# The last block of an attention and experts kernel: an early half projection, zero products, rounded products first, one add on GpSimd

## What is computed

```python
h = layernorm(x) * (1 + ca) + sa
q, k, v = split(h @ W_attn + b_attn)                 # 16 heads of 16
phi = exp(x_head @ omega - |x_head|^2 / 2)           # 128 features
y = (phi_q . cumsum(phi_k v)) / (phi_q . cumsum(phi_k) + eps)
x = x + ga * (y @ W_proj + b_proj)
h = layernorm(x) * (1 + cb) + sb
w = the two largest of softmax(h @ Wg.T + bg), else 0
out = sum over experts e: w[e] * (relu(h @ Wi.T + (h @ A[e].T) @ B[e].T) @ Wo.T)
x = x + gb * out
```

## Time and profile before

| what | value |
| --- | --- |
| median of 3 runs | 759.66 us (759.54 to 762.26) |
| the profiled execution | 758.48 us, its span 756.4 us |
| TensorE matmul busy | 736.2 us, 97% of the span |
| DVE busy | 517.0 us, 68% |
| ScalarE busy | 428.4 us, 57% |
| GpSimd busy | 72.2 us, 10% |

### The profile page before, as it was taken

The page is one execution under the profiler, slowest core; times in us unless marked ns, Lnnn a source line. Parts: engine busy times, 40 slices in busy tenths (PEclk is TensorE's granted clock), DMA queues, the critical chain, the costliest instruction groups (busy, mean ns, idle before and its releaser), DMA issues.

```text
span 756.4 us, 16898 instructions
## 1 busy us (share of the span) xinstructions
PE 736.2 (97%) x6074; PEld 594.8 (79%) x6074; DVE 517.0 (68%) x1255; ACT 428.4 (57%) x775; POOL 72.2 (10%) x81
## 2 busy tenths in 40 slices
PE   8999999999999999999999999999999999999697
PEld 5778779887788868887698877987788876988466
DVE  5647777577667777677766776667766777666566
ACT  4767455765566646665547655666366645565232
POOL 0560200002000110002000020000200010000200
PEclk9999999999999999999999999999999999999899
DMA  9750660107410272104701064101731038000000
GB/s 308 230 116 2 167 155 21 35 28 199 92 55 0 83 184 52 55 0 141 178 0 55 28 194 97 55 0 58 185 75 55 0 118 190 11 30 27 3 1 29
DMA packets 33929, 62.66 MB, mean 83 GB/s; under 512 B 3694, under 2 KB 17874, under 8 KB 33842
## 3 DMA queue, kind: packets, MB, share of 16 engines
q1 hardware_dynamic: 33334, 61.09, 30.7%
q10 hardware_dynamic: 576, 1.31, 0.5%
HBM read 40.37 MB, written 22.02 MB: 82 GB/s over the span
## 4 chain that ended last, share of the span: by engine, by line
PE 87%; DVE 5%; DMA 3%; SPq 2%; ACT 1%; issue 1%; POOL 0%; ACTq 0%; DVEq 0%
PE pa L535 13%; PE ring L658 11%; PE prod L548 7%; PE ring L514 6%; PE pa L410 5%; PE pa L411 5%; PE pa L412 5%; PE ring L568 4%; PE pa L646 4%; PE ring L519 3%; DMA xq<-norm_parts 3%; PE ring L732 2%; PE ring L575 2%; PE prod L514 2%; PE ring L724 2%; PE ring L680 2%
## 5 line engine op out<-in xcount | busy, mean ns | idle before, releaser
L1169 DVE TENSOR_TENSOR am_phk<-pa,const 128x512 f32<-128x512 f32 x112 | 77.1, 689 | 44.3 <-PE pa L535 43.5
L535 PE MATMUL pa<-phq,phkT 128*128 128x128 f32 x768 | 101.2, 275 | 0.0
L535 PEld LDWEIGHTS pa<-phq,phkT 128*128 128x128 f32 x768 | 95.4, 191 | 2.1
L1348 DVE SCALAR_TENSOR_TENSOR am_phk<-ring,am_phk 128x512 f32<-128x512 f32 x64 | 44.1, 689 | 48.2 <-PE ring L732 48.2
L514 PE MATMUL ring<-xq,omega_x 100*128 100x512 f32 x198 | 71.1, 439 | 2.6 <-DMA xq<-norm_parts 1.6
L410 PE MATMUL pa<-wo_r,qk_r 128*128 128x256 f32 x256 | 72.1, 282 | 0.6 <-DVE qk_l L1353 0.6
L411 PE MATMUL pa<-wo_r,qk_l 128*128 128x256 f32 x256 | 72.0, 281 | 0.0
L412 PE MATMUL pa<-wo_l,qk_r 128*128 128x256 f32 x256 | 71.9, 281 | 0.0
L897 ACT ACTIVATE phq<-ring 128x512 f32<-128x512 f32 x84 | 50.6, 602 | 37.4 <-PE ring L514 36.3
L975 ACT ACTIVATE qk_r<-phq 128x512 fp32r<-128x512 f32 x64 | 40.5, 633 | 49.9 <-DVE phq L1357 49.9
L897 ACT ACTIVATE phkT<-ring 128x512 f32<-128x512 f32 x98 | 58.3, 595 | 13.3 <-PE ring L514 12.9
(11 more groups left out here) (201 smaller groups left out, 1596.3 us busy)
## 6 DMA issues: line engine op xcount, KB each, us to landing
xq<-qk_parts SPq DMA_DIRECT2D x45, 512.0 KB
qk_parts<-qk_r SPq DMA_DIRECT2D x32, 256.0 KB, 3.6
qk_parts<-qk_l SPq DMA_DIRECT2D x32, 256.0 KB, 3.9
xr<-in_L_attn_x SPq DMA_DIRECT2D x8, 512.0 KB, 3.5
out_x<-tg SPq DMA_DIRECT2D x16, 256.0 KB, 2.2
tok<-in_L_attn_x SPq DMA_DIRECT2D x7, 512.0 KB, 3.5
phq<-in_L_wmod SPq DMA_DIRECT2D x2, 512.0 KB, 7.4
am_phk<-in_wi_columns SPq DMA_DIRECT2D x2, 512.0 KB, 8.9
```

The source lines that it names most:

```text
L535: mm = pe.matmul(score_bank(q, a)[:, tt], phkT[:, q % 2, a, tt], query(q)[:, a, tt], start=True, stop=True)
L1169: dve.tensor_tensor(am[:, 2 * (q % 2) + a, :].rearrange("p (c t) -> p c t", c=NT), score_bank(q, a)[:].rearrange("p (c t) -> p c t", c=NT) ...
L1348: dve.scalar_tensor_tensor(r2[:, f % 2, :], z_bank[f % 4][:], 0.0, rho, ALU.max, ALU.mult).then_inc(r2_done.sem, 1)
```

## The change

All of it concerns the last block.

1. y's first half is transposed ahead of the last `state_transpose` and copied by ScalarE behind its last copy of products. Its share of the projection is formed in two parts: the first pair of tiles ahead of the last `state_reads`, the second pair ahead of the last `out_transpose`. Behind the attention only k = 1 is left.
2. Three calls of the zero product (`warm(3)`) stand behind the projection.
3. In the last two chunks TensorE takes the eight products of the rounded sums first (`late_output`) and then the four of the difference, each set with a wait of its own. DVE forms the last chunk's sum before the difference of the chunk before it.
4. In `finish` GpSimd adds x to the first pair of tiles, and SyncE waits for it by the new signal `last_first`.

The first hunk is on SyncE, then come TensorE, ScalarE (`copy`), DVE (`late`, `continue`) and GpSimd. `last_stores` is called in place of `ffn_stores` for the last block.

```diff
+            def last_stores(n):
+                    if b == 0:
+                        sp.wait_ge(last_first.sem, 1)
+                    else:
+                        wait(sp, fin, n, 1)
...
                     out_transpose(n, gr - 1)
+                    if q >= PAIRS and not front_next:
+                        y_transpose(n, 0)
...
+                if not front_next:
+                    project(n, 0, 0)
                 state_reads(n, GROUPS - 1)
                 if front_next:
                     qk(n + 1, 2, [1])
+                else:
+                    project(n, 1, 0)
                 out_transpose(n, GROUPS - 1)
...
+                for half in range(2):
+                    for k in range(KT) if front_next else (1,):
+                        project(n, half, k)
...
+            def late_output(n, k):
+                out_of = lambda t: pa[t // 2][:, t % 2 * C:(t % 2 + 1) * C]
+                wait(pe, g_high, n, k + 1)
+                for t in range(NT):
+                    for w in (wo_r, wo_l):
+                        pe.matmul(out_of(t), g_r[:, k % 3, t * P:(t + 1) * P], w[:, k, :], start=False, stop=False,
+                                  skip_group_check=True)
+                wait(pe, g_low, n, k + 1)
+                for t in range(NT):
+                    mm = pe.matmul(out_of(t), g_l[:, k % 3, t * P:(t + 1) * P], wo_r[:, k, :], start=False,
+                                   stop=k == FT - 1, skip_group_check=True)
+                    if k == FT - 1 and t == 1:
+                        mm.then_inc(wo_first.sem, 1)
+                mm.then_inc(wo_mm.sem, 1)
...
-                        wait(pe, g_low, n, k + 1)
+                        if front_next or k < FT - 2:
+                            wait(pe, g_low, n, k + 1)
+                        else:
+                            late_output(n, k)
+                            continue
...
                     qk(n + 1, 3, [1])
                     values(n + 1)
+                else:
+                    warm(3)
                 ffn_head(n, front_next)
...
                     copy(gr)
+                    if gr == GROUPS - 1 and not front_next:
+                        y_copy(n, [0])
...
+                late = FT if front_next else FT - 1
...
-                    if f >= 1:
-                        k = f - 1
-                        wait(dve, g_high, n, k + 1)
-                        dve.tensor_tensor(g_l[:, k % 3, :], g[:, k % 4, :], g_r[:, k % 3, :].bitcast(F32),
-                                          ALU.subtract).then_inc(g_low.sem, 1)
+                    if f >= 1 and f != late:
+                        low_gated(n, f - 1)
                     if f < FT:
                         wait(dve, r2_done, n, f + 1)
                         dve.tensor_tensor(g[:, f % 4, :], g[:, f % 4, :], r2[:, f % 2, :],
                                           ALU.add).then_inc(g_sum.sem, 1)
+                    if f == late:
+                        low_gated(n, f - 1)
...
+                    if b == 0 and not front_next:
+                        continue
                     wait(dve, scaled, n + 1, 2 * b + 2)
...
             rstd_by_halves(NB - 1)
+            wait(pool, scaled, NB, 2)
+            pool.tensor_tensor(tg[:, 0, :], tg[:, 0, :], xr[:, 0:2, :].rearrange("p t c -> p (t c)"),
+                               ALU.add).then_inc(last_first.sem, 1)
```

More of the change, by code:

```diff
@@ L257, in build @@
         oT_added, o_ps, y_step = sig("oT_added", GROUPS), sig("o_ps", GROUPS), sig("y_step", 3 * GROUPS)
+        last_first = sig("last_first")
         mod2_set, mod1_set, mod2c_set = sig("mod2_set", 1), sig("mod1_set", 1), sig("mod2c_set", 2)
@@ L388, in ffn_stores @@
                                  tg[:, b, :].rearrange("p (t c) -> p t c", t=2)).then_inc(out_done.sem, 16)
+            def last_stores(n):
+                dst = block_rows(out_rows, n)
+                for b in range(2):
+                    if b == 0:
+                        sp.wait_ge(last_first.sem, 1)
+                    else:
+                        wait(sp, fin, n, 1)
+                    sp.dma_start(dst[:, 2 * b:2 * b + 2, :],
+                                 tg[:, b, :].rearrange("p (t c) -> p t c", t=2)).then_inc(out_done.sem, 16)
             first_front()
@@ L400, in _ @@
             load_xr(NB - 1)
-            ffn_stores(NB - 1)
+            last_stores(NB - 1)
             wait(sp, out_done, NB, out_done.per)
@@ L638, in projection, with project @@
                     wait(pe, qk_split, n + 1, 2)
+                for half in range(2):
+                    for k in range(KT) if front_next else (1,):
+                        project(n, half, k)
+            def project(n, half, k):
                 row = n // BLOCKS_PER_ROW
[L640 to L647, removed]
+                wait(pe, yT_done, n, k + 1)
+                w = wp_ga[:, row, k, :] if isinstance(n, int) else \
+                    wp_ga[:, bass.ds(row, 1), k, :].rearrange("p o c -> p (o c)")
+                for t in (2 * half, 2 * half + 1):
+                    mm = pe.matmul(pa[half][:, t % 2 * C:(t % 2 + 1) * C], yT[:, k, t * P:(t + 1) * P], w,
+                                   start=k == 0 and t % 2 == 0, stop=k == KT - 1, skip_group_check=True)
+                if k == KT - 1:
                     mm.then_inc(prj_ps.sem, 1)
@@ L788, in after_attend @@
             def after_attend(n, front_next):
-                y_transpose(n, 0)
                 if front_next:
+                    y_transpose(n, 0)
                     qk(n + 1, 3, [0])
@@ L924, in attend, with y_copy @@
                                 front_hT(n + 1)
-            def y_copy(n):
-                for k in range(KT):
+            def y_copy(n, ks):
+                for k in ks:
                     wait(act, yT_ps, n, k + 1)
@@ L1002, in after_attend @@
                     front_qk(n + 1, 2)
-                y_copy(n)
+                y_copy(n, range(KT) if front_next else [1])
                 if front_next:
@@ L1341, in mask_low, with experts @@
                 dve.tensor_tensor(low_both, low, pa[1][0:LROWS], ALU.mult).then_inc(low_masked.sem, 1)
-            def experts(n):
+            def experts(n, front_next):
                 wait(dve, rho_done, n, 1)
+                late = FT if front_next else FT - 1
                 for f in range(FT + 1):
@@ L1358, in experts, with low_gated, finish @@
                                           ALU.add).then_inc(g_sum.sem, 1)
-            def finish(n):
+                    if f == late:
+                        low_gated(n, f - 1)
+            def low_gated(n, k):
+                wait(dve, g_high, n, k + 1)
+                dve.tensor_tensor(g_l[:, k % 3, :], g[:, k % 4, :], g_r[:, k % 3, :].bitcast(F32),
+                                  ALU.subtract).then_inc(g_low.sem, 1)
+            def finish(n, front_next):
                 for b in range(2):
@@ L1383, in ffn_rest @@
                 dve.reciprocal(w1[:], wsum[:]).then_inc(rt.sem, 1)
-                experts(n)
-                finish(n)
+                experts(n, front_next)
+                finish(n, front_next)
             setup_constants()
```

## The result

The changed kernel took 754.9 us (median of 4 executions, 754.69 to 757.15) beside 760.5 for the kernel before, timed with it. The ratio is 0.9947, interval 0.993 to 0.9964: 0.53% or, on the 759.66 shown above, 4.0 us faster, which gives 755.6. Its profiled execution was the longest of the four, 757.15 with a span of 754.8; the other three spans are 752.3 to 752.5. That difference of 2.3 to 2.5 us within one kernel is as large as what the change was forecast to bring, and most of the experiments are about it.

A forecast was written before the change was run, and what follows sets the result against it. TensorE holds 87% of the last-ending chain, so the question was how much of the last block's roughly 50 us is waiting. 1.0 + 0.1 + 0.7 + 0.6 = 2.4 us off 759.66 gives 757.3 us; range 755.3 to 760.2.

The forecast's parts named there:

- the two terms that hang on the clock: Last block: gain of 1.0 us at the attention's end and 0.7 us at the logits, from TensorE's clock staying up.
- the first rival: Last block: clock stays up throughout, logits save 1.8 us, gain 3.55, 756.1 us; chance 0.2.
- the forecast's own case: Ahead of or in the logits: a clock fall costs part of their 1.80 us saving, 0.7 taken; chance 0.35.
- The attention's end: Last block: early half projection fills idle TensorE, last transposes take 0.66 us each, residual starts about 708.7; gain 1.0 us.
- bounds of 0.2 and 1.0: Attention's end: gain 0.2 us from fewer instructions behind the copy alone, up to 1.0 if the clock also stays up.
- The 0.2 for less work behind the copy: Attention's end: four instead of eight instructions behind ACT's copy bring DVE's first projected pair at 709.5, not 709.70.
- The zeros: Behind the projection: three zero calls cost nothing at full clock and save 0.7 us of a possible 1.80 at the logits.
- My ground for 0.7: Ahead of the logits: four microseconds nearly empty, only eight transposes, is closer to what made the clock fall before.
- the end of that cover: Layernorm's transposes: zeros are hidden if over by 712.55; at the low clock they take 5.4 us, over 2 us late.
- The tail: Last two chunks to end: new order and GpSimd's add together gain 0.6 us; bounds 0 and 1.1.
- 0.57: Tail: rounded products first give DVE its first half at 750.2, not 750.77; gain stated as 0.6 us, bounds 0 and 0.7.
- the two causes that I gave: Tail: second store's data queues behind the first's; DVE's last add may wait for GpSimd's until 752.5, ending at 753.2.

The follow-up runs named there:

- e4: Kernel before with the tail alone: order of the last two chunks and GpSimd's add with its store; ratio to before 0.9991 (0.9976 to 1.0006).
- e2: Kernel before with the three zero products behind the projection and nothing else; ratio to before 0.9963 (0.9946 to 0.9981).
- e8: Kernel before with the new order of the last two chunks alone, both adds on VectorE; ratio to before 1.0001 (0.9977 to 1.0025).
- e10: Changed kernel with the early half projection replaced by one zero product in each of its two places; ratio to before 0.9955 (0.9938 to 0.9971).
- e3: Kernel before with the early half projection alone; ratio to before 0.9976 (0.9963 to 0.999).
- e11: Changed kernel with six zero products, warm(6), in place of three; ratio to before 0.996 (0.9941 to 0.9979).
- e5: Changed kernel with the first pair's add back on VectorE; ratio to before 0.9926 (0.9897 to 0.9954).
- e6: Changed kernel with 24 transposes of the identity in place of the three zero products; ratio to before 0.9945 (0.9927 to 0.9963).
- e1: Changed kernel without the three zero products; ratio to before 0.998 (0.9963 to 0.9998).
- e9: Changed kernel timed again without any edit, on another chip; ratio to before 0.9949 (0.9929 to 0.997), median span 754.95 us.

## Why the prediction was right in kind and short in size

The forecast was 2.4 us faster with a part of the logits at the low clock; measured are 4.0 by the ratio (2.7 to 5.3 by its interval). The time was in the range when the ratio is put on the 759.66 shown; the changed kernel's own median of 754.9 is 0.4 below it. So it is the width of the range that held, not its middle: the two terms that hang on the clock came out too small against most of the traces. Most traces went by the first rival, the clock up throughout the last block, for which I had 756.1 and a chance of 0.2; the forecast's own case, a fall that costs part of the logits, is in the first trace alone, where the clock fell at 716.1 and 0.2 of the 1.8 were saved.

*The attention's end, 1.0 forecast, 0.9 to 2.5 measured.* The mechanism is right step by step: 0.66 for 1.12 and 1.11, the residual 0.1 behind GpSimd's add. The sum was made against one execution in which the low clock ended as the projection started (12.95 to the residual). Of the four traces with the old attention end three are longer, 13.89, 14.54 and 14.54: there the clock is back only behind most of the projection (at 710.4, 711.5 and 710.6 in e4, e2 and e8), not at 707.8, at its start. The new end takes 12.06 to 12.18 in nine of ten traces (e10's filled one among them), 12.75 in e3. That bounds of 0.2 and 1.0 were taken from one trace of a clock that I myself had called not tied to the program is the step that failed: the upper bound should have been 2.5. The 0.2 for less work behind the copy is nothing (e10).

*The zeros, 0.7 of 1.8 forecast.* The term of the sum that was mis-sized. Of the eight traces with zeros ahead of the layernorm, seven have the logits at 2.02, one (the changed kernel's first) at 3.59; of the five without, none. So it was worth 1.8 in seven traces of eight and 0.2 in one. My ground for 0.7, that the 4 us ahead of the logits are nearly empty, was not borne out: in these seven traces the clock stayed up through them. That the zeros are hidden was right: 2.74 us for six, over before the first transposes in the changed kernel; and so was the end of that cover (e11).

*The tail, 0.6 forecast, 0.5 measured.* 0.57 was worked out for the order, 4.54 to 4.03 came, and all of it reaches the end (e8). For GpSimd's add little was left in my sum; it is 0.02 to 0.14 (e5). Of the two causes that I gave, the queue of the second store's data fits the rows of e5 (2.4 us to landing instead of 2.1). The DVE add that comes second was delayed by 0.38 us; the data of the store in front covers that, by the same rows, but no run takes the delay away alone. The two stores were issued about 0.55 us apart, not within 0.5.

*Two readings of mine.* The clock is back at 721.4, not at 721.2: the last row is low for most of its half microsecond. Nothing hangs on it. And that no row has the DVE add second is wrong. Setup has one, DVE's L1163 with two SBUF operands, begun inside a GpSimd instruction that reads SBUF:

```profile
26.48 1.95 POOL L1448 TENSOR_SCALAR tok<-xr 128x512 f32<-128x512 f32 x1 [15.93 <-ACT xr L837]
27.37 1.23 DVE L1163 TENSOR_TENSOR wo_l<-am_phk,wo_r 128x1024 fp32r<-128x1024 f32 x1 [1.25 <-ACT wo_r L876]
```

It takes 1.23 us, undisturbed 1.22 (the same line at 24.06), so here it did not wait at all.

*The Trainium skill on both points.* "TensorE: Matmul & The Clock Gate", Part 4, has it that transposes don't count for the clock as matmuls do. The runs are against it: in e6 24 transposes stand where the zeros stood, and the clock held as with them. "SBUF — State Buffer" (Who interferes with whom) has it that a VectorE instruction with two SBUF operands waits for a GpSimd one that reads SBUF to end: the add that was ready at 750.88 ended at 751.95, which is 0.55 after GpSimd's end at 751.40; 0.69 would be a full wait. For these two adds the trace agrees nearly; for the pair in setup above it does not.

Added up, 12.95 - 12.06, 3.81 - 2.02, 0.14 from the transposes ahead of the logits (7.41 to 7.27) and 0.5 make 3.3 us against the profiled execution, and 5.5 against e8's trace: 14.54 - 12.06, 3.82 - 2.02, 26.0 - 25.3 behind the logits, which my sum had nowhere, and 0.5. The measured 4.0 lies between. What stays open is how often each fall happens; for that the traces, one a kernel, are too few.

## What to carry to other kernels

Look at where the clock is low in the last, unoverlapped block before anything else: there the engine idles between dependent steps, and work of no use, put where it waits anyway, can be worth more than moving real work (here 2.4 of some 4 us, by the ratios of e1 and e9, which are from two chips). Fit it to end before what stands behind it in the queue is ready. Two stores that become ready together cost within 0.14 us as much here as one that is ready early and one late; and a single trace of a part with such a clock is one draw, so compare stages over several traces before sizing a gain.

## What the runs showed of the hardware that was not expected

The clock's falls are not the same from execution to execution of one kernel, in setup too: the changed kernel's two traces reach the same instruction at 696.96 and 699.04, and 90 executions of the kernel before span 755.0 to 762.6 us. Not all of it is the clock: from the first block's residual to the last block's last but one add of reads it is full in every trace, and this takes 608.96 to 610.56 us. 24 transposes in 2.78 us keep TensorE's clock at its full level as well as six instructions of zero products in 2.74 do.
